# Macaron block (FFN, state-space scan, FFN) on Trainium2: two block-scale products move from VectorE to GpSimd, and all four lists are reordered

## The reference

```python
x = x + 0.5 * ffn(layernorm(x))      # pass A
x = x + scan(layernorm(x))           # stage S
x = x + 0.5 * ffn(layernorm(x))      # pass C
```

```python
scale = maximum(max(abs(xb)) / 6.0, 1e-12)       # one per block of 16
q = GRID[searchsorted(MID, abs(xb / scale))] * sign(xb) * scale
```

## Time and profile before

| | |
|---|---|
| Median of 3 runs | 4114.31 us (4113.19 to 4118.74) |
| The profiled execution | 4118.5 us |
| Its span, first to last instruction | 4116.8 us |
| VectorE (DVE) busy | 3740.5 us, 91% |
| TensorE (PE) busy | 3662.4 us, 89% |
| ScalarE (ACT) busy | 3191.1 us, 78% |
| GpSimd (POOL) busy | 2154.0 us, 52% |
| TensorE clock granted, mean | 0.97 |

### The profile page before, as it was taken

The page is one execution under the profiler, slowest core; times in us unless marked ns, Lnnn a source line. Parts: engine busy times, 40 slices in busy tenths (PEclk is TensorE's granted clock), DMA queues, the critical chain, the costliest instruction groups (busy, mean ns, idle before and its releaser), DMA issues. The chain is left out here.

```text
span 4116.8 us, 81697 instructions
## 1 busy us (share of the span) xinstructions
PE 3662.4 (89%) x29740; PEld 2754.3 (67%) x29740; DVE 3740.5 (91%) x6358; ACT 3191.1 (78%) x6115; POOL 2154.0 (52%) x1779
## 2 busy tenths in 40 slices
...
GB/s 28 11 11 17 7 13 15 17 16 17 6 17 12 17 16 17 17 6 12 16 16 17 17 7 17 11 17 16 17 17 6 12 16 17 17 17 6 11 11 11
DMA packets 46452, 57.93 MB, mean 14 GB/s; under 512 B 7463, under 2 KB 41704, under 8 KB 46056
## 3 DMA queue, kind: packets, MB, share of 16 engines
...
...
## 5 line engine op out<-in xcount | busy, mean ns | idle before, releaser
L793 DVE TENSOR_TENSOR_SCAN state<-w_ps,decay 128x512 f32<-128x512 f32 x1024 | 1212.9, 1213 | 13.3 <-ACT decay L999 9.2
L1120 PE MATMUL gu_ps<-wgu,qxT 128*128 128x352 f16 x6144 | 1037.0, 319 | 116.7 <-DVE hid L717 78.8
L1120 PEld LDWEIGHTS gu_ps<-wgu,qxT 128*128 128x128 f16 x6144 | 572.6, 99 | 513.1 <-DVE hid L717 126.9
L1186 PE MATMUL w_ps<-bdif,x_parts 128*128 128x129 f16 (+1 forms) x12288 | 866.5, 224 | 46.4 <-DVE state L793 22.8
L1186 PEld LDWEIGHTS w_ps<-bdif,x_parts 128*128 128x128 f16 x12288 | 782.1, 99 | 137.5 <-issue 101.8
L1127 PE MATMUL td_ps<-wd,qhT 128*128 128x256 f32 x3072 | 736.1, 390 | 4.3 <-ACT qhT L920 4.2
L803 DVE SCALAR_TENSOR_TENSOR c_state<-state,inv_A,rep_ps 128x512 f32<-128x512 f32 x1024 | 726.2, 736 | 0.3
L999 ACT ACTIVATE decay<-dt,A_sb 128x512 f32<-128x512 f32 x1024 | 685.2, 718 | 17.7 <-DVE state L793 13.5
L464 POOL TENSOR_TENSOR val<-val,magic 128x704 f32<-128x704 f32 x256 | 408.7, 1597 | 499.3 <-DVE magic L737 499.3
L989 ACT ACTIVATE bdif<-dif,B_tok 128x129 f16<-128x129 f16 x2048 | 642.4, 397 | 18.9 <-DVE B_tok L759 18.9
L1127 PEld LDWEIGHTS td_ps<-wd,qhT 128*128 128x128 f32 x3072 | 570.1, 192 | 90.7 <-issue 14.0
...
## 6 DMA issues: line engine op xcount, KB each, us to landing
...
```

Source lines behind the costliest of these rows:

```text
L793: v.tensor_tensor_scan(state[:, n % 2, gi, :], w_ps[:, gi, :], decay[:, n % 2, gi, :], 0.0, ALU.add, ALU.mult).then_inc(state_ready.sem, 1)
L1120: last = te.matmul(gu_ps[:, m, 0:FH], qxT[:, t // 2, 4 * (t % 2) + xp * G + c], wgu[:, c, wp, a:a + FH], start=begin, stop=end)
L1186: last = te.matmul(w_ps[:, gi, t * P:t * P + wide], x_parts[:, xp, t, gi * P:(gi + 1) * P], bdif[:, n % NB, t, bp, 0:wide], start=(t, xp, ...
```

## The change

`xv` and `qp` leave VectorE's list and its functions and appear in GpSimd's, with the same operands, shapes and semaphores. Two waits are new on VectorE: the h scales wait until qh of the pass before has been made (scale is read by GpSimd now), and a scan from state 2 on waits for the product that read its buffer. In the four lists the same pieces stand in another order.

```diff
@@ GpSimd
+            def values_x(q, k):
+                rows = slice(k * (T // 2), (k + 1) * (T // 2))
+                cols = slice(k * (T // 2) * DM, (k + 1) * (T // 2) * DM)
+                pool.wait_ge(qx_step.sem, qx_step.at(q, 6))
+                if not first(q):
+                    pool.wait_ge(grid_x.sem, grid_x.at(q - 1, 2 * k + 2))
+                by = x_recip[:, k * (T // 2) * XB_:(k + 1) * (T // 2) * XB_].rearrange("p (t b) -> p t b", b=XB_)
+                g.tensor_tensor(x_val[:, cols].rearrange("p (t i b) -> p t i b", i=BLOCK, b=XB_),
+                                f_xh[:, rows, :].rearrange("p t (b i) -> p t i b", i=BLOCK),
+                                by.unsqueeze(2).broadcast_to([P, T // 2, BLOCK, XB_]),
+                                ALU.mult).then_inc(x_val_ready.sem, 1)
...
+            def quantised_h(q, t):
+                if not first(q):
+                    pool.wait_ge(tr_full.sem, tr_full.at(q - 1, HP * t + HP))
+                pool.wait_ge(grid_h.sem, grid_h.at(q, 2 * t + 2))
+                g.tensor_tensor(qh[:, t, 0:F].rearrange("p (b i) -> p b i", i=BLOCK),
+                                grid[:, t % 2].rearrange("p (b i) -> p b i", i=BLOCK),
+                                scale[:, t * HB:(t + 1) * HB].unsqueeze(2).broadcast_to([P, HB, BLOCK]),
+                                ALU.mult).then_inc(qh_ready.sem, 1)
@@ VectorE: values_x and quantised_h are taken out, and
             def scales_h(q, half):
...
+                if not first(q):
+                    dve.wait_ge(qh_ready.sem, qh_ready.at(q - 1, 2 * half + 2))
                 v.tensor_scalar(scale[:, s], amax[:, s], 1.0 / 6.0, MIN_SCALE, ALU.mult,
                                 ALU.max).then_inc(qh_step.sem, 1)
...
             def state_of(seq, m):
...
+                if n >= 2:
+                    dve.wait_ge(c_state_ready.sem, c_state_ready.at(seq, m - G + 1))
                 dve.wait_ge(w_ready.sem, w_ready.at(seq, G + m + 1))
```

```diff
 PE
-    A.gu0 A.gu1 A.gu2 S.xt0 A.gu3 S.rb0 S.bt0 A.gu4 A.gu5 S.z0 S.k0 S.k1 S.w0 S.w1 S.c0 A.gu6 A.gu7 A.ht0 S.e0
-    S.e1 A.ht1 A.ht2 S.w2 S.w3 A.dn0 S.c1 S.w4 C.tx0 S.p0 A.ht3 S.p1 S.p2 A.ht4 S.w5 A.ht5 S.c2 C.tx1 A.dn1 S.w6
...
+    A.gu0 A.gu1 A.gu2 S.xt0 A.gu3 S.rb0 A.gu4 S.bt0 A.gu5 S.z0 S.c0 S.k0 S.k1 A.gu6 S.e0 S.e1 S.w0 S.w1 A.gu7
+    A.ht0 A.ht1 C.tx0 A.ht2 S.w2 A.dn0 S.w3 S.w4 A.ht3 S.c1 S.p0 S.p1 A.ht4 S.w5 S.p2 A.ht5 S.c2 C.tx1 A.dn1
...
 DVE
-    S.ln0 A.hid0 C.ln0 A.hid1 A.am0 A.hid2 C.xa0 C.xa1 C.xs0 C.xv0 C.xv1 C.xm0 A.hid3 A.am1 S.cb0 S.tb0 A.qs0
-    A.hid4 S.sc0 S.k0 S.k1 A.qm0 A.hid5 C.xm1 A.am2 S.dt0 A.hid6 A.qp0 C.qy0 A.qm1 S.g0 S.g1 S.p0 S.p1 S.g2 S.g3
...
+    S.ln0 A.hid0 C.ln0 A.hid1 A.am0 A.hid2 C.xa0 C.xa1 C.xs0 A.hid3 A.am1 A.qs0 C.xm0 S.cb0 A.hid4 S.tb0 S.sc0
+    A.qm0 S.k0 S.k1 A.hid5 S.dt0 A.hid6 A.am2 C.qy0 C.xm1 A.qm1 A.hid7 S.g0 A.am3 S.p0 S.g1 S.g2 A.res0 S.p1
...
 ACT
-    A.gu0 A.gu1 S.ln0 A.gu2 C.ln0 S.xt0 A.gu3 S.xh0 C.ax0 S.rb0 C.ax1 A.gu4 S.b0 S.b1 A.gu5 A.ah0 S.z0 A.gu6
-    A.ah1 S.d0 A.ht0 S.d1 A.ht1 S.b2 A.ht2 S.d2 S.d3 A.gu7 S.d4 S.d5 A.ht3 S.d6 A.ht4 A.ht5 S.b3 S.b4 C.tx0
...
+    A.gu0 A.gu1 S.ln0 A.gu2 C.ln0 S.xt0 A.gu3 C.ax0 S.rb0 A.gu4 S.xh0 A.ah0 A.gu5 S.b0 S.z0 A.gu6 A.ah1 C.ax1
+    A.gu7 S.d0 A.ht0 S.b1 A.ht1 S.d1 A.ht2 S.d2 S.d3 S.b2 S.b3 S.b4 A.ht3 A.ht4 C.tx0 A.ht5 S.d4 S.d5 S.d6 S.d7
...
 POOL
-    S.ln0 C.ln0 C.mx0 A.mv0 A.mv1 S.xl0 S.bl0 S.bl1 A.mh0 A.mh1 S.bl2 S.bl3 C.mx1 A.mv2 A.mv3 S.bl4 S.bl5 S.bl6
-    A.mh2 A.mh3 S.bl7 S.bl8 S.bl9 C.mv0 C.mv1 C.mh0 C.mh1 S.bl10 S.bl11 S.bl12 S.bl13 C.mv2 S.bl14 C.mh2 C.mv3
-    N.ln0 C.mh3 S.bl15 N.mx0 N.mx1
+    S.ln0 C.ln0 C.xv0 C.xv1 A.mv0 S.bl0 S.bl1 A.mv1 C.mx0 S.xl0 A.mh0 A.qp0 A.mh1 S.bl2 A.qp1 C.mx1 S.bl3 A.mv2
+    A.mv3 S.bl4 S.bl5 S.bl6 S.bl7 A.mh2 A.qp2 A.mh3 S.bl8 S.bl9 C.mv0 C.mv1 A.qp3 C.mh0 S.bl10 C.qp0 C.mh1
+    S.bl11 S.bl12 C.mv2 C.mv3 S.bl13 N.ln0 C.qp1 C.mh2 S.bl14 C.qp2 C.mh3 N.xv0 N.xv1 C.qp3 S.bl15 N.mx0 N.mx1
```

More of the change, by code:

```diff
@@ new lines @@
+    S.w6 S.w7 C.gu0 S.w8 S.w9 S.c3 S.p3 C.gu1 C.gu2 S.w10 S.p4 S.c4 C.gu3 S.p5 S.w11 S.p6 S.w12 A.ht6 S.p7 S.c5
+    C.gu4 S.w13 A.ht7 S.p8 S.w14 S.c6 A.ht8 S.p9 S.p10 S.w15 C.gu5 A.dn2 S.c7 S.p11 S.w16 A.ht9 S.p12 S.w17 S.c8
+    C.gu6 A.ht10 S.p13 S.p14 S.w18 S.w19 A.ht11 S.c9 C.gu7 S.p15 A.dn3 S.w20 S.w21 C.ht0 S.p16 S.p17 C.ht1 S.p18
+    S.p19 C.ht2 S.c10 S.w22 C.dn0 S.w23 S.w24 C.ht3 S.p20 S.p21 C.ht4 S.c11 S.w25 C.ht5 S.w26 C.dn1 S.w27 S.c12
+    C.ht6 S.p22 S.p23 C.ht7 S.w28 S.c13 C.ht8 S.p24 S.p25 C.dn2 S.w29 S.c14 C.ht9 S.p26 S.p27 C.ht10 S.w30 S.w31
@@ L37 @@
+    C.ht11 S.c15 S.p28 C.dn3 N.tx0 N.tx1 S.p29 S.p30 S.p31
     """,
     "DVE": """
-    S.ln0 A.hid0 C.ln0 A.hid1 A.am0 A.hid2 C.xa0 C.xa1 C.xs0 C.xv0 C.xv1 C.xm0 A.hid3 A.am1 S.cb0 S.tb0 A.qs0
-    A.hid4 S.sc0 S.k0 S.k1 A.qm0 A.hid5 C.xm1 A.am2 S.dt0 A.hid6 A.qp0 C.qy0 A.qm1 S.g0 S.g1 S.p0 S.p1 S.g2 S.g3
-    A.hid7 A.res0 A.qp1 S.p2 A.am3 S.p3 C.qy1 A.qs1 S.g4 S.g5 S.p4 S.p5 S.g6 S.g7 S.p6 A.qm2 S.p7 S.g8 C.hid0
-    S.g9 A.res1 A.qp2 A.qm3 C.hid1 S.p8 S.p9 C.am0 C.hid2 S.g10 S.g11 S.p10 S.p11 C.hid3 S.g12 C.am1 S.p12 A.qp3
@@ new lines @@
+    A.qm0 S.k0 S.k1 A.hid5 S.dt0 A.hid6 A.am2 C.qy0 C.xm1 A.qm1 A.hid7 S.g0 A.am3 S.p0 S.g1 S.g2 A.res0 S.p1
+    S.g3 S.p2 S.p3 C.qy1 A.qs1 S.g4 S.g5 S.p4 S.g6 S.g7 S.p5 S.g8 C.hid0 S.g9 A.qm2 C.hid1 A.res1 S.p6 S.p7
+    C.am0 C.hid2 S.g10 S.p8 A.qm3 C.hid3 S.p9 C.am1 S.g11 S.g12 S.p10 S.p11 S.g13 C.qs0 C.hid4 S.p12 S.p13 S.g14
+    C.hid5 S.g15 C.qm0 A.res2 S.p14 S.p15 C.am2 S.g16 S.g17 S.p16 S.p17 C.qm1 C.hid6 S.g18 S.g19 S.p18 C.hid7
+    S.p19 C.am3 C.qs1 A.res3 S.g20 S.g21 N.ln0 S.p20 S.g22 S.p21 C.res0 C.qm2 C.qm3 S.g23 S.g24 N.xa0 S.p22
@@ L57 @@
+    S.d8 C.tx1 A.ah2 S.d9 S.d10 C.gu0 S.b5 C.gu1 S.b6 C.gu2 S.b7 S.b8 A.ah3 C.gu3 S.d11 S.d12 S.d13 S.d14 S.d15
+    A.ht6 C.gu4 A.ht7 S.b9 S.b10 A.ht8 S.b11 C.gu5 C.ah0 C.ah1 S.d16 S.d17 S.d18 S.d19 A.ht9 C.gu6 A.ht10 A.ht11
+    S.b12 C.gu7 S.b13 S.d20 S.d21 S.d22 C.ht0 C.ht1 C.ht2 C.ah2 S.d23 C.ah3 S.d24 S.d25 N.ln0 C.ht3 C.ht4 C.ht5
+    S.d26 S.b14 S.b15 S.d27 C.ht6 S.d28 C.ht7 C.ht8 N.ax0 N.ax1 S.d29 C.ht9 S.d30 S.d31 C.ht10 C.ht11 N.tx0
+    N.tx1
     """,
     "POOL": """
-    S.ln0 C.ln0 C.mx0 A.mv0 A.mv1 S.xl0 S.bl0 S.bl1 A.mh0 A.mh1 S.bl2 S.bl3 C.mx1 A.mv2 A.mv3 S.bl4 S.bl5 S.bl6
@@ L483, in body @@
                         low_b(unit["S"], k)
+                    elif step == "xv":
+                        values_x(unit[stage], k)
                     elif step == "mx":
@@ L489, in body @@
                         round_h(unit[stage], k)
+                    elif step == "qp":
+                        quantised_h(unit[stage], k)
             body(-1, order("POOL", "N"), None, None, 0)
```

38 lines of the change are left out of this document (2 added, 36 removed).

## The result

| | before | after |
|---|---|---|
| Median of 5 runs each | 4114.31 us (4110.94 to 4118.74) | 4087.75 us (4080.30 to 4096.72) |
| Ratio | | 0.9936 [0.9922, 0.9951] |
| Span of the profiled execution | 4116.8 us | 4085.6 us |
| Mean of the 29 full periods | 121.7 us | 120.77 us |
| Front, scan part (means) | 31.2, 90.5 us | 33.2, 87.6 us |

The change gains 0.64%, clear of noise (the interval ends at 0.9951), where 4.9% was forecast; the median lies above the range of 3800 to 4065 us. A period loses 0.93 us, and 29 times that is the whole difference of 27 us. The front of a period is counted from the first statistics instruction of stage S to the first scan, the scan part is the rest.

A forecast was written before the change was run, and what follows sets the result against it. A chain-bound front and a scan part bound by VectorE's work: 31 + 84 = 115 us a period, 6.7 less; 29 periods (194 us) and 8 us more give 202 us off, about 3913 us; range 3800 to 4065 us.

The forecast's parts named there:

- 7.6 + 3.9 = 11.5 us a period: VectorE: eight qh (7.6 us) and four x_val (3.9 us) leave it each period, so it needs 103.0 us.
- Costs of the moved instructions: GpSimd: qh 1.39 us each, x_val 1.7 us (bounds 1.01 and 1.94); its work rises to 84.9 us a period.
- Table loads, TensorE's need: ScalarE's table changes fall from 15 to 11 a cycle; TensorE needs 81.1 us in the scan part.
- The front stays at 31 us: the relief of VectorE buys nothing here: Front, before the first scan: a chain through several engines sets it, so it stays at 31 us.
- rival C: Slower through shared access of VectorE and GpSimd at magic, x_magic, first qx; twelve more hits cost 10.2 us, 4215 us; chance 0.12.
- GpSimd waits for most of these instructions, so they start when it is idle: Argument against more VectorE-GpSimd collisions at magic, x_magic and the first qx, sixteen instructions a period.
- A scan part of about 90 us that is VectorE's own work: From the first scan on, VectorE, busy 98%, is the limit; this part shrinks when work leaves it, to 84 us.
- I add 1 us for that and 1 us for more VectorE instructions that meet a busy GpSimd: Scan part: 1 us for TensorE-VectorE hand-overs with two buffers, 1 us for collisions, on top of 82.7 us.
- A: VectorE's relief comes through in full: period 110.5 us, 11.2 less, 3790 us; chance 0.13.
- B: Most of the gain goes into latency of GpSimd's queue: period 119 to 120, 4050 us; chance 0.17.
- D: GpSimd's strided x_val read far dearer than 1.94 us; at 4 us the front grows 4.6 us; no chance of its own.
- no difference: Whole kernel: time within 0.2%, some 8 us, of no change; chance 0.03.

The follow-up runs named there:

- e12: Kernel after with GpSimd's x_val product reading f_xh densely instead of with a step of 16 elements: 4049.53 us, 0.9845 of before.
- e4: Kernel after with both moved products (x_val and qh) back on VectorE, so the new lists alone: 4408.65 us, 1.0727 of before.
- e7: Kernel after with dt made by one VectorE instruction with a PSUM input, upper clip bound left out, direct part of y later on TensorE: 4045.6 us.
- e8: Kernel after with C.xv1 moved behind A.mv0 in GpSimd's list: 4057.31 us, 0.9870 of before.
- e9: Kernel after with dt made by one VectorE instruction from PSUM and C.xv1 moved behind S.bl1 in GpSimd's list: 4014.02 us, 0.9758 of before.
- e15: Kernel before with product p (the product with C) made for half the tokens, 8.6 us a period off VectorE: 4069.89 us, 0.9898 of before.
- e1: Kernel after with one more wait: GpSimd's first rounding of h waits until dt is made: 4154.47 us, 1.0108 of before.
- e10: Kernel after with the statistics of N three pieces later on VectorE only: 4186.43 us, 1.0186 of before.
- e11: Kernel before's lists with both products on GpSimd, each behind the piece it needs: 4183.74 us, 1.0172 of before.

## Why the prediction was wrong, point by point

The sum said 31 + 84 = 115; measured are 33.2 + 87.6 = 120.8. Of the 5.8 us missing, 2.2 are in the front and 3.6 in the scan part.

**"7.6 + 3.9 = 11.5 us a period" off VectorE: too much by 1.8.** The records of instructions that follow each other overlap, by 0.07 to 0.09 us on either side of the two products, so taking them out frees less than their durations. The durations on VectorE add up to 418.1 us more than its busy time before and to 359.8 more after.

**Costs of the moved instructions: right.** qh 1.387 us at the median (1.39 said), 1.48 in the mean, since a few wait for VectorE. x_val 1.52, between the bounds of 1.01 and 1.94 and below the 1.7 taken. The transfer of VectorE's factor of 1.67 to GpSimd was the weak point: measured is 1.19. The estimate by the Trainium skill (GPSIMD Engine Reference, Performance pitfalls for Q7 kernels) was 1.44, nearer than my 1.7; but e12 shows 1.27 dense plus 0.24 for the step, not my 1.01 plus its 0.43, so two errors cancel in it. GpSimd is busy 84.2 us a period (84.9 said).

**Table loads, TensorE's need: right.** ScalarE has 124 instructions fewer, four a period. TensorE's shortest distances between starts add up to 81.3 us in the scan part of after (81.1 said).

**"The front stays at 31 us: the relief of VectorE buys nothing here": the step that failed first.** The chain to dt was judged well: dt starts 26.0 us into the front, 0.6 earlier than before (26.6), in spite of the scale's 1.34 us more. But I priced the meeting with GpSimd at x_magic alone, and rival C's list of sixteen instructions (magic, x_magic, the first qx) left out dt, its clip and the h scales. These three hold 3.4 of the 4.4 us a period that VectorE has above the forecast 103.0: dt 38.0 us, its clip 31.1, the scale 41.0 of the whole span (the difference of the two groups each; of before the scale has 25.4 us, dt 39.5 and the clip 23.0), while magic fell by 12.4. Most of the rest is the overlap above. "GpSimd waits for most of these instructions, so they start when it is idle" was said of magic and is not true of these three. Nor was it the moved work alone: e4 has dt's 1.2 us, and a front of 33.4 us, from the new lists with neither product moved. The prediction goes through the front with the new order of VectorE and ScalarE, and nowhere asks beside which GpSimd piece dt will stand. Of the small pieces that I said share something with GpSimd, only the scale did: hid3 and am1 never took more than 0.59 and 0.89 us. e7 takes away dt's meeting, e8 the scale's and e9 both, and the front is 31.7, 32.8 and 30.9 us against 33.2. The Trainium skill (SBUF — State Buffer, Who interferes with whom) has the rule that I cited for rival C: two-input and two-port work in SBUF excludes GpSimd. The trace agrees for dt, clip and scale (2.53, 1.76, 1.55 us), and by e7 the same length with one input in PSUM is 1.22. I had the rule and a row for it, and did not go through the front with it instruction by instruction.

**"A scan part of about 90 us that is VectorE's own work. Only the second one shrinks by itself when work leaves VectorE": wrong.** e15 is the test: 8.6 us off, 1.5 gained. TensorE's shortest steps add up to 81.5 us there in before, and to them come about 4.5 us in gaps under 0.15 us and 4.3 us of waits and issue; it was nearly as full as VectorE, and my subtraction took the shortest steps, found in a stretch without waits, for what a stretch with waits would need.

**"I add 1 us for that and 1 us for more VectorE instructions that meet a busy GpSimd": the term mis-sized.** The scan part is 6.3 us longer than TensorE's 81.3: about 4 in gaps under 0.15 us, 0.8 at the lower granted clock, 0.6 waiting for state, the rest in waits of 0.2 to 0.4 us a period for single pieces. Before it was 9.0 over 81.5, none of it at the lower clock. The change took 2.7 us of that.

**The rivals.** A fell: no relief came through in full. C was the right mechanism at a third of its size (3.4 us a period for its 10.2) and at other instructions. B is near in time (4050) by luck, and wrong in place: after's lists avoid the latency, and e1, e10 and e11 show what it costs where they don't. D is out: 1.52 us.

The result lies close to "no difference", to which I gave 0.03. The chances came from asking which engine has slack, not which hand-overs have it.
